# TensorE transposes one pair of edge tiles ahead instead of two (graph attention and expert layer, one core)

## The chip, the core and the metric

The kernel runs on one NeuronCore of a Trainium2 chip. TensorE (PE in the rows, PEld its weight loads) multiplies matrices into PSUM, VectorE is DVE, ScalarE is ACT, GpSimd is POOL, SyncE is SP. The time is the device time of one execution in microseconds, the median of several runs. Lower is better.

## What is computed

A graph network with three layers of message passing over 3125 nodes and 50000 edges, then a mixture of 8 experts over the nodes. Nearly all of the time that matters here goes into the messages of the three layers:

```
Q, K, V = (h @ Wq.T + bq), (h @ Wk.T + bk), (h @ Wv.T + bv)      # 4 heads of 64, for each node
scores  = einsum('ehd,egd->ehg', Q[src], K[tgt]) / 8             # 4x4 for each edge
attn    = softmax(scores, axis=-1)
msg     = einsum('ehg,egd->ehd', attn, V[tgt]) + Ee[edge_type]
proj    = msg @ Wo.T + bo
m       = segment_sum(proj, src)                                 # by source node
h       = relu(layer_norm(h + m, ln_g, ln_b))
```

## The kernel before, in words

The kernel sorts the edges by source node once. It groups them in tiles of 128 edges whose sources lie in one window of 16 nodes. `kv_d` in HBM holds a row of 512 numbers per node: 256 of K and 256 of V. In each of the three layers the edge phase (`e_phase`) walks over all tiles, two tiles (a **pair**) at a time. There are 294 pairs in a layer, 882 in all. Twelve pairs make a **turn** (`PAIRS` = 12). The first and the last turn are written out, and the turns between are a hardware loop on every engine. The last turn is a half one with 6 pairs, so a layer has 24 turn ends, 72 in all.

The order of the work on each engine is written out by hand, and semaphores tie the engines together. For a pair p:

- **POOL** gathers the 128 rows of each of its two tiles from `kv_d` into `kv` with two indirect DMAs (L527). `kv` holds 12 pairs. So the gathers of the next turn's pair p may start only after the aggregation of this turn's pair p (`agg_done`).
- **PE, `keys`** (L1463 to L1469) waits for `gathered` and transposes the K half of both tiles into bank 3 + p % 2: 4 transposes. It raises `kT_done`.
- **ACT, `keys`** (L1242 to L1245) copies that bank to `kt_s[:, p % 2]` and raises `kT_ready`. Behind it in ACT's order stand the four small copies of `queries` for the next pair (L1239, L1240), and after every fourth pair the exponentials of a group of four pairs (`exps`, L1249), which wait for DVE.
- **PE, `scores`** (L1471 to L1483) first multiplies a bf16 mask into bank p % 3 (L1474), then waits for `kT_ready` and multiplies `kt_s` by the block diagonal queries `qbd`: 4 products (L1481). It raises `score_done`.
- **DVE** takes maxima (`best`, L763), and for a group of four pairs makes the softmax. It spreads the weights to `att` (L789), and adds the result of the aggregation to the window's sums `acc` (`add`, L806).
- **PE, `aggregate`** (L1485 to L1494) multiplies the V half of the tiles by `att`: 8 products into bank 5 + p % 3. It runs 7 pairs behind the scores (`LAG` = 7) and raises `agg_done`, for which DVE's `add` and POOL's gathers wait.

An fp32 product is two matmul records in the trace, so a pair counts 1 mask product, 8 scores records and 16 aggregation records; the 4 transposes count 4.

The loop over pairs in PE's `turn` (L1502 to L1509) is where the change is. In the kernel before, `keys` for pair p + 1 stands ahead of `aggregate` and `scores` of pair p. Before the first turn stands `keys(0)` (L1511).

Of the kernel before, what the change touches and what calls it, by code (L numbers as in the profile page):

```python
# [49 lines left out]
PAIRS = TILES // 2  # L50
# [3 lines left out]
LAG = 7  # L54
# [29 lines left out]
def build(nc, A, out):  # L84
    ctx = ExitStack()
    with ctx:
# [1291 lines left out]
        def _(pe):  # L1378
# [83 lines left out]
            def e_phase(l):  # L1462
                def keys(p, landed):  # L1463
                    for t in (2 * p, 2 * p + 1):
                        pe.wait_ge(gathered[t], landed)
                        for c in range(KC):
                            o = (t % 2) * D + c * P
                            ins = pe.transpose(bank[3 + p % 2][:, o:o + P], kv[:, t // UB, t % UB, c * P:(c + 1) * P], ident[:, :])  # L1468
                    ins.then_inc(S.kT_done, 1)  # L1469

                def scores(i, p, at):  # L1471
                    bk = bank[p % 3]
                    pe.wait_ge(S.score_read, at[p + 1])
                    mm(bk[:, :], ohT[:, ds(i * (PAIRS // 4) + p // 4, 1), :].squeeze(1),  # L1474
                       maskc[:, 2 * (p % 4):2 * (p % 4) + 2, :].unsqueeze(2).to_broadcast([P, 2, H, DH]),
                       start=True, stop=False, skip_group_check=True)
                    pe.wait_ge(S.kT_ready, at[p])
                    for u in range(2):
                        for c in range(KC):
                            o = u * D + c * P  # L1480
                            ins = mm(bk[:, o:o + P], kt_s[:, p % 2, u, c, :], qbd[:, p % 4, u, :],  # L1481
                                     start=False, stop=(c == KC - 1), skip_group_check=True)
                    ins.then_inc(S.score_done, 1)  # L1483

                def aggregate(p, weights, read):  # L1485
                    pe.wait_ge(S.att_ready, weights)
                    pe.wait_ge(S.chain_b, read)
                    for g in range(H):
                        for t in (2 * p, 2 * p + 1):
                            b, u, r = t // UB, t % UB, t % 2 * DH  # L1490
                            ins = mm(bank[5 + p % 3][r:r + DH, 0:DH], kv[:, b, u, D + g * DH:D + (g + 1) * DH],  # L1491
                                     att[:, b % 2, u, :, g, :],
                                     start=(g == 0), stop=(g == H - 1), skip_group_check=True)
                    ins.then_inc(S.agg_done, 1)  # L1494

                def turn(i, first, last):
                    pairs = LASTP if last else PAIRS
                    at = [pe.snap(l * EP + i * PAIRS + p + 1) for p in range(pairs + 1)]
                    read = [pe.snap(l * EP + i * PAIRS + p) for p in range(pairs)]
                    here = [pe.snap((l * (NTURN - h) + i + 1) * 16) for h in range(2)]  # L1500
                    ahead = pe.snap((l * NTURN + i + 2) * 16)
                    for p in range(pairs):  # L1502
                        if p + 1 < pairs:
                            keys(p + 1, here[(p + 1) * 2 // PAIRS])
                        elif not last:
                            keys(0, ahead)
                        if p >= LAG or not first:
                            aggregate((p - LAG) % PAIRS, at[p], read[p])
                        scores(i, p, at)  # L1509

                keys(0, pe.snap((l * NTURN + 1) * 16))  # L1511
                turn(0, True, False)
# [294 lines left out]
```

## Time and profile before

| | |
|---|---|
| time, median of 3 runs | 4428.94 us (4425.26 to 4429.85) |
| span of the profiled execution | 4428.6 us |
| PE busy | 3650.6 us, 82% of the span |
| DVE busy | 2620.2 us, 59% |
| POOL busy | 2316.9 us, 52% |
| ACT busy | 2195.7 us, 50% |
| three edge phases | 953, 951 and 952 us, from their first to their last scores |
| DMA in the edge phases | 161 GB/s, 58% of the 16 engines |

The profiled execution is as long as the median run. The three edge phases are 2856 us of it, 3.24 us for each of the 882 pairs. PE is recorded as busy for about 83% of an edge phase. Its matmuls overlap each other in the records, and the record of one tells when it was issued and a modelled end.

### The profile page before, as it was taken

The numbers are of one execution on the slowest core, as the hardware profiler recorded it, in microseconds if no ns is written. First come the engines' busy times: TensorE is split into PE (matmuls) and PEld (weight loads), VectorE is DVE, ScalarE is ACT, GpSimd is POOL, SyncE is SP. The second block draws the span as 40 slices with busy tenths as digits, with TensorE's granted clock in tenths as the row PEclk, the third lists the DMA queues.
The fourth block names the chain that finished last, engine by engine and source line by source line (L and its number), as shares of the span: only waits on it lengthen the run. The fifth ranks groups of instructions, "written<-read, shape, count | busy, mean of one in ns | idle before, by whom it ended". The sixth has DMA issues, their size and how long they took to land.

```text
span 4428.6 us, 98340 instructions
## 1 busy us (share of the span) xinstructions
PE 3650.6 (82%) x32539; PEld 2873.4 (65%) x32540; DVE 2620.2 (59%) x6787; ACT 2195.7 (50%) x6662; POOL 2316.9 (52%) x2354
## 2 busy tenths in 40 slices
PE   5777878888888887888888888788888888868999
PEld 2333547676766664776667676567666667657998
DVE  6555626676666753666667665367666667661111
ACT  3667755454444434554445543455544445323443
POOL 2555225666666633566666663356666666334444
PEclk9777889999999988999999998899999999888999
DMA  2000145555555534555555553455555555436665
GB/s 65 0 0 0 39 156 145 163 162 162 163 163 161 163 95 151 150 161 163 161 164 163 163 161 94 137 157 161 163 163 163 163 162 162 131 108 186 186 181 127
DMA packets 231295, 611.20 MB, mean 138 GB/s; under 512 B 52352, under 2 KB 96269, under 8 KB 222862
## 3 DMA queue, kind: packets, MB, share of 16 engines
q0 software_dynamic: 161376, 477.59, 39.7%
q1 hardware_dynamic: 69822, 132.43, 8.9%
q8 instruction: 46, 0.75, 0.1%
q14 instruction: 51, 0.42, 0.0%
HBM read 562.97 MB, written 47.19 MB: 138 GB/s over the span
## 4 chain that ended last, share of the span: by engine, by line
PE 75%; issue 13%; DVE 6%; another core or an unknown queue 3%; DVEq 1%; ACT 1%; DMA 1%; SPq 0%; POOL 0%; ACTq 0%; POOLq 0%
PE bank L1481 19%; PE bank L1491 15%; PE bank L1468 9%; PE bank L1474 6%; PE bank L1680 5%; PE bank L1692 4%; PE bank L1452 3%; PE bank L1525 2%; PE bank L1404 2%; PE bank L1418 2%; PE bank L1446 2%; PE bank L1412 1%; PE bank L1420 1%; PE bank L1526 1%
## 5 line engine op out<-in xcount | busy, mean ns | idle before, releaser
L527 POOL DMA_INDIRECT arena<-kv_d,gidx x1764 | 1754.7, 995 | 1283.2 <-PE bank L1491 541.5
L1481 PE MATMUL bank<-qbd,kt_s 128*128 128x128 f32 x7056 | 1063.7, 289 | 173.2 <-issue 119.9
L1481 PEld LDWEIGHTS bank<-qbd,kt_s 128*128 128x128 f32 x7056 | 1014.2, 203 | 261.5 <-issue 183.1
L1244 ACT ACTIVATE kt_s<-bank 128x512 f32<-128x512 f32 x882 | 523.7, 594 | 1207.3 <-PE bank L1468 583.9
L1491 PE MATMUL bank<-att,arena 128*64 128x64 f32 x14112 | 777.2, 237 | 275.0 <-issue 227.9
L763 DVE TENSOR_REDUCE sc<-bank 128x32 f32<-128x512 f32 x882 | 610.0, 692 | 661.4 <-remote 331.9
L1491 PEld LDWEIGHTS bank<-att,arena 128*64 128x64 f32 x14112 | 588.0, 144 | 493.4 <-issue 449.9
L789 DVE TENSOR_TENSOR att<-at_s,arena 128x512 f32<-128x512 f32 x882 | 610.8, 692 | 57.8 <-DVE at_s L782 23.8
L1468 PE MATMUL bank<-ident,arena 128*128 128x128 f32 x3528 | 586.2, 286 | 68.8 <-issue 41.8
L806 DVE TENSOR_TENSOR arena<-bank,arena 64x64 f32 x1764 | 393.6, 223 | 222.0 <-issue 85.0
L1468 PEld LDWEIGHTS bank<-ident,arena 128*128 128x128 f32 x3528 | 444.8, 149 | 98.4 <-issue 86.9
L1239 ACT ACTIVATE qbd<-arena 64x64 f32 x1764 | 441.5, 250 | 56.2 <-issue 45.7
L1240 ACT ACTIVATE qbd<-arena 64x64 f32 x1764 | 449.4, 255 | 20.5
L511 POOL DMA_INDIRECT rec_d<-arena x241 | 242.9, 1008 | 255.7 <-DVE arena L713 184.8
L1474 PE MATMUL bank<-maskc,arena 128*128 128x512 bf16 x882 | 358.0, 406 | 22.4 <-issue 21.9
L699 DVE CUSTOM_DVE_ANT_0 arena<-bank,arena 128x200 f32<-128x200 f32 x391 | 138.5, 363 | 176.5 <-PE bank L1418 88.2
L1151 DVE TENSOR_TENSOR arena<-bank,arena 128x256 f32<-128x256 f32 x56 | 23.8, 425 | 357.5 <-PE bank L1692 357.5
L1680 PE MATMUL bank<-xT,arena 128*128 128x128 f32 x1792 | 211.9, 277 | 0.0
L1680 PEld LDWEIGHTS bank<-xT,arena 128*128 128x128 f32 x1792 | 207.2, 194 | 0.4 <-ACT xT L1359 0.4
L1412 PE MATMUL bank<-arena 128*128 128x200 bf16 x391 | 112.7, 299 | 112.9 <-DVE rank L699 78.7
L1692 PE MATMUL bank<-arena 128*128 x896 | 202.6, 379 | 0.0
L1171 ACT ACTIVATE arena<-arena 128x592 bf16<-128x592 f32 x150 | 105.1, 776 | 176.1 <-DVE arena L716 168.6
(239 smaller groups left out, 3845.4 us busy)
## 6 DMA issues: line engine op xcount, KB each, us to landing
arena<-in_pack SPq DMA_DIRECT2D x56, 1030.0 KB
arena<-kv_d,gidx POOLq DMA_INDIRECT x1764
kv_d<-arena SPq DMA_DIRECT2D x50, 256.0 KB, 2.0
xin<-hid_d SPq DMA_DIRECT2D x75, 128.0 KB
arena<-in_w SPq DMA_DIRECT2D x8, 1024.0 KB, 6.1
kv_d<-arena SPq DMA_DIRECT2D x5, 1280.0 KB, 5.3
hid_d<-arena SPq DMA_DIRECT2D x50, 128.0 KB, 2.0
rec_d<-arena POOLq DMA_INDIRECT x241
```

The costliest lines, as they stand in the source:

```text
L527: pool.indirect_dma_start(kv[:, t // UB, t % UB, :], None, kv_d, bass.IndirectOffsetOnAxis(gidx[:, h, t - h * HT:t - h * HT + 1], 0),).the ...
L763: dve.tensor_reduce(sc[:, 2 * m:2 * m + 2], bank[q % 3][:, :].rearrange("p (t g s h) -> p t g h s", t=2, g=H, s=W), AX.X, ALU.max).then_in ...
L789: dve.tensor_tensor(att[:, b, u:u + 2].rearrange("p t s g h -> p t s (g h)"), at_s[:, 2 * m:2 * m + 2].rearrange("p t g h -> p t (g h)").u ...
L806: dve.tensor_tensor(a.rearrange("p (h s) -> p h s", h=H), bank[5 + p % 3][u * DH:(u + 1) * DH, 0:DH].rearrange("p (s h) -> p h s", h=H), a ...
L1239: act.activation(qbd[0:DH, p % 4, u, 0:64], q, ACT.Copy)
L1240: act.activation(qbd[DH:P, p % 4, u, 64:128], q, ACT.Copy)
L1244: act.activation(kt_s[:, p % 2], bank[3 + p % 2][:, :].rearrange("p (u c n) -> p u c n", u=2, n=P), ACT.Copy).then_inc(S.kT_ready, 1)
L1468: ins = pe.transpose(bank[3 + p % 2][:, o:o + P], kv[:, t // UB, t % UB, c * P:(c + 1) * P], ident[:, :])
L1474: mm(bk[:, :], ohT[:, ds(i * (PAIRS // 4) + p // 4, 1), :].squeeze(1), maskc[:, 2 * (p % 4):2 * (p % 4) + 2, :].unsqueeze(2).to_broadcast( ...
L1481: ins = mm(bk[:, o:o + P], kt_s[:, p % 2, u, c, :], qbd[:, p % 4, u, :], start=False, stop=(c == KC - 1), skip_group_check=True)
L1491: ins = mm(bank[5 + p % 3][r:r + DH, 0:DH], kv[:, b, u, D + g * DH:D + (g + 1) * DH], att[:, b % 2, u, :, g, :], start=(g == 0), stop=(g = ...
L1680: ins = mm(bank[1 + 2 * (p % 2) + h // 4][:, (h % 4) * P:(h % 4 + 1) * P], w1s[:, p, c * HID + h * P:c * HID + (h + 1) * P], xT[:, p % 2, ...
```

## The change

PE's loop over the pairs now takes `aggregate` and `scores` first and `keys` last. All three calls, their operands, banks and semaphore waits are the same as before, and so are the other engines' programs.

```
--- before.py
+++ after.py
@@ -1500,13 +1500,13 @@
                     here = [pe.snap((l * (NTURN - h) + i + 1) * 16) for h in range(2)]
                     ahead = pe.snap((l * NTURN + i + 2) * 16)
                     for p in range(pairs):
+                        if p >= LAG or not first:
+                            aggregate((p - LAG) % PAIRS, at[p], read[p])
+                        scores(i, p, at)
                         if p + 1 < pairs:
                             keys(p + 1, here[(p + 1) * 2 // PAIRS])
                         elif not last:
                             keys(0, ahead)
-                        if p >= LAG or not first:
-                            aggregate((p - LAG) % PAIRS, at[p], read[p])
-                        scores(i, p, at)
 
                 keys(0, pe.snap((l * NTURN + 1) * 16))
                 turn(0, True, False)
```

The first place is inside the hardware loop on PE, between two pairs. `gathered4` and `gathered5` are the landings of pair 2's tiles, `kT_ready` is ACT's copy of the transposed keys. Before, from the transposes of pair 2 on, the next products are:

```order
L1468 MATMUL bank<-ident,arena 128x128 [waits gathered4]
L1468 MATMUL bank<-ident,arena 128x128
L1468 MATMUL bank<-ident,arena 128x128 [waits gathered5]
L1468 MATMUL bank<-ident,arena 128x128
L1491 MATMUL bank<-att,arena 64x64 [waits chain_b,att_ready]
L1491 MATMUL bank<-att,arena 64x64 x7
L1473 REGISTER_ALU
L1474 MATMUL bank<-maskc,arena 128x512 [waits score_read]
L1481 MATMUL bank<-qbd,kt_s 128x128 [waits kT_ready]
L1481 MATMUL bank<-qbd,kt_s 128x128 x3
```

The scores in these rows are those of pair 1, so the scores of pair 2 come one whole round later. After, from the transposes of pair 1 on:

```order
L1468 MATMUL bank<-ident,arena 128x128 [waits gathered2]
L1468 MATMUL bank<-ident,arena 128x128
L1468 MATMUL bank<-ident,arena 128x128 [waits gathered3]
L1468 MATMUL bank<-ident,arena 128x128
L1491 MATMUL bank<-att,arena 64x64 [waits chain_b,att_ready]
L1491 MATMUL bank<-att,arena 64x64 x7
L1473 REGISTER_ALU
L1474 MATMUL bank<-maskc,arena 128x512 [waits score_read]
L1481 MATMUL bank<-qbd,kt_s 128x128 [waits kT_ready]
L1481 MATMUL bank<-qbd,kt_s 128x128 x3
```

The round reads the same, but here the transposes are those of pair 1 (`gathered2`, `gathered3`), like the scores. The transposes have moved behind the previous pair's scores, and only one aggregation and one mask product stand between a pair's transposes and its scores.

The second place is the start of a layer on PE. Before, two pairs are transposed ahead of the first scores:

```order
L1468 MATMUL bank<-ident,arena 128x128 [waits gathered0,oht_copied]
L1468 MATMUL bank<-ident,arena 128x128
L1468 MATMUL bank<-ident,arena 128x128 [waits gathered1]
L1468 MATMUL bank<-ident,arena 128x128
L1468 MATMUL bank<-ident,arena 128x128 [waits gathered2]
L1468 MATMUL bank<-ident,arena 128x128
L1468 MATMUL bank<-ident,arena 128x128 [waits gathered3]
L1468 MATMUL bank<-ident,arena 128x128
L1474 MATMUL bank<-maskc,arena 128x512 [waits score_read]
L1481 MATMUL bank<-qbd,kt_s 128x128 [waits kT_ready]
L1481 MATMUL bank<-qbd,kt_s 128x128 x3
```

After, the first scores follow the first pair's transposes directly:

```order
L1468 MATMUL bank<-ident,arena 128x128 [waits gathered0,oht_copied]
L1468 MATMUL bank<-ident,arena 128x128
L1468 MATMUL bank<-ident,arena 128x128 [waits gathered1]
L1468 MATMUL bank<-ident,arena 128x128
L1474 MATMUL bank<-maskc,arena 128x512 [waits score_read]
L1481 MATMUL bank<-qbd,kt_s 128x128 [waits kT_ready]
L1481 MATMUL bank<-qbd,kt_s 128x128 x3
L1468 MATMUL bank<-ident,arena 128x128 [waits gathered2]
L1468 MATMUL bank<-ident,arena 128x128
L1468 MATMUL bank<-ident,arena 128x128 [waits gathered3]
L1468 MATMUL bank<-ident,arena 128x128
```

Here the transposes of pair 1 (`gathered2`, `gathered3`) have moved behind the scores of pair 0.

## Rows read from the trace of the kernel before

**Rows 1.** The page: busy time by engine, and the costliest group of instructions.

```profile
PE 3650.6 (82%) x32539; PEld 2873.4 (65%) x32540; DVE 2620.2 (59%) x6787; ACT 2195.7 (50%) x6662; POOL 2316.9 (52%) x2354
...
L527 POOL DMA_INDIRECT arena<-kv_d,gidx x1764 | 1754.7, 995 | 1283.2 <-PE bank L1491 541.5
```

**Rows 2.** Windows, the edge phases: length, busy us by engine, clock, DMA share, GB/s.

```profile
639.00:1592.00 953.00, 789.26 (x8400) 660.08 (x8399) 644.11 (x1512) 467.25 (x1582) 581.14 (x582) 0.93 0.58 161
...
2846.00:3798.00 952.00, 781.83 (x8402) 651.02 (x8401) 643.60 (x1509) 465.79 (x1581) 575.41 (x582) 0.95 0.57 161
```

**Rows 3.** Line 527, POOL's gathers: what ended POOL's idle time (us, times).

```profile
  PE bank L1491: 541.5, 311
  issue: 484.2, 1382
...
  remote: 125.3, 70
```

**Rows 4.** Line 1244, ACT's copy of the keys: what it waited for (us, times).

```profile
  PE bank L1468: 583.9, 240
  remote: 578.4, 224
```

**Rows 5.** Timeline around two pairs that pass undisturbed: start, duration, idle before.

```profile
1508.58 1.05 PE L1481 MATMUL bank<-qbd,kt_s 128*128 128x128 f32 x8
...
1509.47 0.60 PE L1468 MATMUL bank<-ident,arena 128*128 128x128 f32 x4
...
1510.00 0.69 PE L1491 MATMUL bank<-att,arena 128*64 128x64 f32 x16
...
1510.11 0.60 ACT L1244 ACTIVATE kt_s<-bank 128x512 f32<-128x512 f32 x1 [0.28 <-issue]
...
1510.62 0.39 PE L1474 MATMUL bank<-maskc,arena 128*128 128x512 bf16 x1
1510.84 1.05 PE L1481 MATMUL bank<-qbd,kt_s 128*128 128x128 f32 x8
```

**Rows 6.** Timeline of a stretch with a late copy.

```profile
1446.59 1.05 PE L1481 MATMUL bank<-qbd,kt_s 128*128 128x128 f32 x8
...
1447.48 0.60 PE L1468 MATMUL bank<-ident,arena 128*128 128x128 f32 x4
...
1448.01 0.69 PE L1491 MATMUL bank<-att,arena 128*64 128x64 f32 x16
...
1448.96 0.38 PE L1474 MATMUL bank<-maskc,arena 128*128 128x512 bf16 x1 [0.26 <-issue]
1449.17 0.60 PE L1481 MATMUL bank<-qbd,kt_s 128*128 128x128 f32 x4
...
1450.39 0.62 PE L1481 MATMUL bank<-qbd,kt_s 128*128 128x128 f32 x4 [0.61 <-issue]
...
1451.84 0.69 DVE L763 TENSOR_REDUCE sc<-bank 128x32 f32<-128x512 f32 x1 [3.66 <-PE bank L1481]
...
1453.26 0.60 ACT L1244 ACTIVATE kt_s<-bank 128x512 f32<-128x512 f32 x1 [5.87 <-PE bank L1468]
```

**Rows 7.** Timeline of POOL alone: the gathers that come after a wait.

```profile
1201.97 1.05 POOL L527 DMA_INDIRECT arena<-kv_d,gidx  x1 [1.04 <-PE bank L1491]
...
1205.56 0.94 POOL L527 DMA_INDIRECT arena<-kv_d,gidx  x1 [1.28 <-PE bank L1491]
...
1212.11 0.94 POOL L527 DMA_INDIRECT arena<-kv_d,gidx  x1 [1.87 <-PE bank L1491]
```

**Rows 8.** Timeline of ACT at a turn's end.

```profile
835.15 0.60 ACT L1244 ACTIVATE kt_s<-bank 128x512 f32<-128x512 f32 x1 [0.24 <-issue]
836.88 0.26 ACT L1239 ACTIVATE qbd<-arena 64x64 f32 x1 [1.13 <-issue]
...
837.95 0.21 ACT L1233 ACTIVATE gidx<-rec 128x12 int32 x1
```

**Rows 9.** Line 1468, PE's transposes: idle time ended by a gather's landing (us, times).

```profile
  DMA arena<-kv_d,gidx: 32.9, 19
```

More of the change, by code:

```diff
@@ L1502, in turn @@
                     for p in range(pairs):
+                        if p >= LAG or not first:
+                            aggregate((p - LAG) % PAIRS, at[p], read[p])
+                        scores(i, p, at)
                         if p + 1 < pairs:
@@ L1506, in turn @@
                             keys(0, ahead)
-                        if p >= LAG or not first:
-                            aggregate((p - LAG) % PAIRS, at[p], read[p])
-                        scores(i, p, at)
                 keys(0, pe.snap((l * NTURN + 1) * 16))
```

## The prediction, made before the changed kernel ran

> **What bounds the kernel now.** I read the page first, then the windows of the three edge phases, then the waits of POOL and ACT, and last two timelines. No engine is full over the span: PE is recorded busy for 82% [rows 1]. The edge phases last 953 and 952 us, with the middle one 2856 us together, or 3.24 us for each of 882 pairs, and PE is busy in 789 of 953 [rows 2]. Where nothing disturbs it, one round is shorter: scores start at 1508.58 and again at 1510.84, so PE needs 2.26 us per pair [rows 5]. 882 x (3.24 - 2.26) = 864 us are lost in the edge phases.
>
> They are not lost where PE visibly waits for data: gather landings end only 32.9 us of idle time in front of the transposes [rows 9]. The late copies tell more. In the undisturbed round the transposes end at 1509.47 + 0.60 = 1510.07, and ACT's copy starts at 1510.11, 0.04 us later [rows 5]. In the other stretch the transposes end at 1448.08 and ACT, idle for 5.87 us, starts the copy at 1453.26, 5.2 us later. The scores that end at 1447.64 are read by an idle DVE only from 1451.84 [rows 6]. So PE's completion signals come late while POOL sends gathers one behind the other. Meanwhile PE's records run on: between the end of those scores and 1451.84 stand 4 + 16 + 1 + 8 matmuls [rows 6], one whole round, and the last of them trickle out with idle gaps of 0.6 us. I take it that PE can run about one round ahead of its own signals and then stands.
>
> With each of these matmuls goes a weight load, so the records are about 58. The Trainium skill ("TensorE: Matmul & The Clock Gate", What a matmul computes and Architectural detail) gives TensorE's queue a depth of 64; by that rule the trace agrees, and the run-ahead would end at 64 records where a dependency doesn't end it earlier.
>
> POOL shows the same from its side. Two gathers are 2 x 0.995 us [rows 1], its short gaps are 484.2 / 882 = 0.55 us per pair, and its waits for an aggregation (541.5 + 125.3 us in 381 times) are 0.76 us per pair [rows 3]: 3.30 us together, the 3.24 us within the rounding of what lies at the phases' ends. One wait comes per 882 / 381 = 2.3 pairs and lasts 1.75 us. So the edge phase beats in bursts: POOL waits, gets the aggregations that have become visible (two or three pairs), sends 4 to 6 gathers, PE's signals stay away meanwhile, and all begins again. How many aggregations a burst finds sets the pace.
>
> **What the change does, part by part.** It removes and adds no instruction. In the steady round the order of kinds stays transposes, aggregation, mask, scores. What moves is the pair: the transposes of a pair run one round, 2.26 us, later against its scores.
>
> (a) The copy in an undisturbed round. Before, from the end of a pair's transposes to its scores there are 2.26 + (1510.84 - 1510.07) = 3.03 us; now 0.77 us. The copy needs 0.04 + 0.60 = 0.64 us [rows 5]. It fits with 0.13 us to spare: the cover is the aggregation and the mask. Cost 0. If the cover is gone (a busy ACT, a late signal), each us of it is a us of PE.
>
> (b) The copy in a disturbed round. Before, a pair's transposes could be hidden from ACT for up to 3.03 - 0.64 = 2.4 us without holding its scores; now for 0.13 us. ACT waited 583.9 + 578.4 us for 464 of 882 copies, 2.5 us each [rows 4]; this is not all lateness of the signal, since ACT is idle between copies anyway. The run-ahead of a whole round ends now at the first scores whose transposes have not become visible, that is after an aggregation and a mask. When the signals come, the copy has to run (0.64 us) before the next scores, and the aggregation behind these comes that much later, near the time when POOL's new gathers shut the signals off again. So a burst finds fewer aggregations. Nothing in the trace of before runs so; I bound it. Low end: the bursts stay as they are, 0. High end: each burst finds one pair. A burst of one pair takes 1205.56 - 1201.97 = 3.59 us [rows 7], against 3.24: 0.35 x 882 = 309 us. A burst of two takes 1212.11 - 1205.56 = 6.55 us [rows 7]. I take the middle, one and two pairs in turn: (3.59 + 6.55) / 3 = 3.38 us per pair, 0.14 x 882 = 124 us. I lean on this one because one aggregation is always in the run-ahead and the next comes about one round plus the copy later (2.9 us), about when a burst of two gathers (2 x 1.25 us) ends.
>
> (c) Turn ends. There ACT loads the windows' registers behind the copy: from the copy's start at 835.15 to the end of the last small operation, 837.95 + 0.21, are 3.01 us [rows 8], against a round of 2.26. The next copy is 0.75 us late, less the 0.13 to spare, where the round is undisturbed. Before, the extra round hid it. I take half, 0.3 us x 72 turn ends = 22 us; ends 0 and 45.
>
> (d) The softmax chain. The exponentials stand behind the copy and the four small copies on ACT, and the copy comes up to one round later. DVE's weights wait for them, and the aggregations wait for DVE's spread. They run 7 pairs behind, so I take 0; if the cover failed it would show as PE waiting at L1491 for L789. I leave up to 50 us for it in the high end.
>
> (e) Gains. The transposes come a round later against their gathers, which can return at most the 32.9 us [rows 9]; most of it lies at the layers' starts, where the landings set the pace in either order. I take 0; ends 0 and -33. The other stages are untouched.
>
> Sum, against the profiled execution (span 4428.6 us, 0.3 below the median 4428.94, so nothing to convert): 4428.6 + 124 + 22 = 4575 us.
>
> **Rivals.**
> One pair per burst: with only 0.13 us to spare every burst finds one aggregation. For it: it takes a signal just 0.13 us late to hold the scores. Against it: after a release two rounds can pass before the signals go (copies come at once in rows 5). 4429 + 309 + 22 = 4760; with (d) and copies that wait as in rows 6, up to 5000.
> The cover holds, not slower: signals are late because PE itself stands, and when it goes on, 0.77 us of aggregation and mask cover 0.64 us of copy just as in the undisturbed round. Then the lookahead was spare, and only (c) could be left. It decides at a copy path of 0.77 us: below it, nothing is lost. 4429, or 4451 with (c). For it: the same order of kinds, the clean round. Against it: the 5.2 us in rows 6.
> By the Trainium skill ("Perfetto Trace Analysis", Matmuls) independent groups should rotate through banks so that the evacuation of one overlaps the next group's products. That rule is still met after the change, and by it the time would be this rival's.
> A faster kernel: the later transposes never meet a gather that hasn't landed, and the first scores of a layer start earlier. 4429 - 33 = 4396. Against it: 19 such waits in 882 pairs [rows 9].
>
> **How the numbers follow.** Middle case 0.46 (4500 to 4660), one pair per burst or worse 0.26 (4660 to 5000), cover holds 0.18, faster 0.10. A difference below 0.2% (9 us) can't be told from none. The cover case gives 0.13 to no change and 0.05 to a small loss by (c), the faster case 0.01 to no change: faster 0.09, same 0.14, slower 0.77. Low end 4425, just at the no-change case; high end 4840, which leaves about 0.1 on each side.
>
> **What would show it.** Right: no change outside the edge phases, each some 50 us longer; more than 381 waits of POOL for an aggregation (near 590), each about as long; PE waiting at L1477's semaphore, idle in front of the scores with ACT's copy as its releaser; recorded run-ahead shorter than a round. (c) is right if intervals at turn ends are the longest. Wrong: POOL's waits as many as before and PE's idle time still in small gaps in the middle of a group; or PE waiting for L789, then (d) was the step. A lower granted clock than 0.93 in an edge phase [rows 2] would be an effect that I left out.

## The result, and the profile after

The changed kernel took 4496.81 us (median of 4 runs, 4491.84 to 4499.76), and the kernel before, on the same chip, 4429.4 us. The ratio is 1.0154, with a 95% interval from 1.0139 to 1.0169: 67 us slower. The forecast was 4575 us, 146 us slower. The sign, the place and the mechanism came out as predicted, the size at less than half of the forecast. The profiled execution of the changed kernel has a span of 4490.0 us, 61.4 more than before.

The page of the changed kernel, busy time by engine and the costliest group. These answer to [rows 1].

```profile
PE 3588.0 (80%) x32539; PEld 2796.1 (62%) x32540; DVE 2621.3 (58%) x6787; ACT 2213.6 (49%) x6662; POOL 2264.2 (50%) x2354
...
L527 POOL DMA_INDIRECT arena<-kv_d,gidx x1764 | 1698.0, 963 | 1404.3 <-PE bank L1491 673.2
```

Windows of the changed kernel: the three edge phases, from their first to about their last scores, against [rows 2] (length, busy us by engine, clock, DMA share, GB/s). The first two end 4.8 and 3.6 us before the last scores do.

```profile
634.00:1606.00 972.00, 765.38 (x8351) 627.37 (x8352) 641.84 (x1505) 471.24 (x1580) 561.83 (x583) 0.95 0.56 158
1761.00:2734.00 973.00, 761.85 (x8372) 626.86 (x8371) 642.91 (x1507) 471.29 (x1580) 559.99 (x581) 0.96 0.56 157
2885.00:3859.00 974.00, 769.04 (x8405) 629.83 (x8406) 644.13 (x1510) 473.62 (x1586) 559.53 (x583) 0.96 0.56 158
```

Counted in the two traces from the first to the start of the last scores, the phases are 23, 25 and 22 us longer, 70 us in all, or 3.32 us a pair in place of 3.24. Counted from a layer's first gather it is 65 us, since the first scores then start 0.7 to 2.3 us earlier (5 us in all). Outside the phases nothing became longer; the first gather came 3.4 us earlier, which leaves the 61.4 of the span. The granted clock is 0.95 and 0.96 where it was 0.93 to 0.95, so it isn't the clock. About 50 of the 65 us are spread over all the later turns (3.29 us a pair between the scores of pairs 12 and 288, before 3.23). Nearly all of the rest, 21 less the 5 that come back, comes in the first turn of each layer.

Now the waits of the same kernel. Line 527, POOL's gathers: what ended the idle time in front of them (us, times), against [rows 3].

```profile
  PE bank L1491: 673.2, 374
  issue: 463.3, 1309
  remote: 135.7, 80
```

Line 1481, PE's scores:

```profile
  ACT kt_s L1244: 529.2, 672
  issue: 320.4, 152
```

Line 1244, ACT's copy of the keys, against [rows 4]:

```profile
  remote: 929.2, 355
  PE bank L1468: 440.6, 487
```

POOL now waits 454 times for an aggregation, 808.9 us, where it waited 381 times, 666.8 us. That is 142 us more. Against it, its gathers are 56.7 us shorter (963 ns in place of 995) and its short gaps 20.9 us (463.3 against 484.2): 142.1 - 56.7 - 20.9 = 64.5 us, the lengthening of the phases counted from their first gathers. PE's idle time in front of the scores (matmuls and weight loads are two rows of the trace and are summed here) ended with ACT's copy 14 times before, for 91.2 us:

The kernel before, line 1481:

```profile
  issue: 303.0, 555
  ACT kt_s L1244: 91.2, 14
```

Now it does so 672 times. The rows don't tell where in a group of eight scores matmuls an idle time lies; the traces do (matmuls alone, idle over 0.15 us). Before, 196 of them, 103.5 us, lay inside a group and only 9, 53.8 us, in front of a group and up to the copy's end. After the change none lies inside a group, and 390, 350.6 us, end within 0.15 us of the copy's end, those that the row calls "issue" among them. The idle time has changed its form as the prediction said: PE no longer runs ahead until its records trickle out, it stands in front of the scores.

The timeline of the changed kernel shows one such round. Columns are start, duration, operation and, in brackets, the idle time before it with its releaser.

```profile
1451.15 0.60 PE L1468 MATMUL bank<-ident,arena 128*128 128x128 f32 x4
...
1451.68 0.69 PE L1491 MATMUL bank<-att,arena 128*64 128x64 f32 x16
...
1452.30 0.10 PEld L1474 LDWEIGHTS bank<-maskc,arena 128*128 x1
1452.30 0.39 PE L1474 MATMUL bank<-maskc,arena 128*128 128x512 bf16 x1
1452.42 1.20 POOL L527 DMA_INDIRECT arena<-kv_d,gidx  x1 [0.30 <-issue]
1452.73 0.60 ACT L1244 ACTIVATE kt_s<-bank 128x512 f32<-128x512 f32 x1 [1.83 <-PE bank L1468]
...
1453.38 1.16 PE L1481 MATMUL bank<-qbd,kt_s 128*128 128x128 f32 x8 [0.69 <-issue]
```

The transposes end at 1451.75, the copy starts 0.98 us later though ACT has been idle for 1.83 us, and the scores follow the copy's end by 0.05 us after PE has stood for 0.69 us. (The row says "issue", but nothing else ends there; only the copy does.) This signal was less late than most; how late they are is counted further down.

### The profile page after: what moved, and what is told of

It is laid out like the page before. It is cut to its first block, busy times and chain, and to the rows that moved or that the text cites. A ratio compares the mean times of both kernels' runs of the same rounds, so it can differ in the third digit from the quotient of the medians.

```text
span 4490.0 us, 98340 instructions
## 1 busy us (share of the span) xinstructions
PE 3588.0 (80%) x32539; PEld 2796.1 (62%) x32540; DVE 2621.3 (58%) x6787; ACT 2213.6 (49%) x6662; POOL 2264.2 (50%) x2354
## 4 chain that ended last, share of the span: by engine, by line
PE 51%; another core or an unknown queue 18%; ACT 13%; issue 9%; DVE 4%; ACTq 3%; DMA 0%; DVEq 0%; SPq 0%; POOL 0%; POOLq 0%
PE bank L1481 14%; PE bank L1468 6%; ACT kt_s L1244 5%; PE bank L1680 5%; PE bank L1692 4%; PE bank L1491 3%; ACT qbd L1240 3%; ACT qbd L1239 3%; PE bank L1452 3%; PE bank L1404 2%; PE bank L1525 2%; ACTq L1259 2%; PE bank L1474 2%; PE bank L1446 2%
## 5 line engine op out<-in xcount | busy, mean ns | idle before, releaser
L527 POOL DMA_INDIRECT arena<-kv_d,gidx x1764 | 1698.0, 963 | 1404.3 <-PE bank L1491 673.2
L1481 PE MATMUL bank<-qbd,kt_s 128*128 128x128 f32 x7056 | 1027.5, 291 | 354.5 <-ACT kt_s L1244 203.4
L1481 PEld LDWEIGHTS bank<-qbd,kt_s 128*128 128x128 f32 x7056 | 900.5, 199 | 520.8 <-ACT kt_s L1244 325.8
L1491 PE MATMUL bank<-att,arena 128*64 128x64 f32 x14112 | 734.1, 235 | 268.8 <-issue 244.3
L1491 PEld LDWEIGHTS bank<-att,arena 128*64 128x64 f32 x14112 | 566.9, 142 | 455.6 <-issue 443.3
L1468 PE MATMUL bank<-ident,arena 128*128 128x128 f32 x3528 | 555.4, 282 | 22.0 <-DMA arena<-kv_d,gidx 22.0
L778 DVE TENSOR_REDUCE sm<-ex 128x32 f32<-128x128 f32 x222 | 83.5, 376 | 199.7 <-ACT ex L1249 186.1
```

Source lines behind the costliest of these rows:

```text
L527: pool.indirect_dma_start(kv[:, t // UB, t % UB, :], None, kv_d, bass.IndirectOffsetOnAxis(gidx[:, h, t - h * HT:t - h * HT + 1], 0),).the ...
```

## The experiments

Sixteen runs followed, of the change once more and of eleven variants. They landed on chips that differ by far more than the change, so each is set against the kernel before on its own chip:

| kernel | order of a pair, or edit | before there | this | ratio (95%) |
|---|---|---|---|---|
| the change | A S(p) K(p+1) | 4429.4 | 4496.81 | 1.0154 (1.0139 to 1.0169) |
| after_2 | the same again | 4431.58 | 4502.49 | 1.0163 (1.0139 to 1.0188) |
| e1_aks_2 | A K(p+1) S(p) | 4431.58 | 4438.11 | 1.0014 (1.0004 to 1.0023) |
| e7_ahead | A K(p+2) S(p) | 4429.86 | 4433.61 | 1.0010 (0.9999 to 1.0021) |
| e8_ahead_exps | e7, exponential earlier | 4429.86 | 4435.11 | 1.0010 (1.0000 to 1.0020) |
| e11_sak | S(p) A K(p+1) | 4509.88 | 4809.45 | 1.0654 (1.0636 to 1.0672) |
| e2_split_2 | the change, copy in halves | 4429.86 | 4528.48 | 1.0232 (1.0214 to 1.0249) |
| e3_exps_2 | the change, exponential earlier | 4429.86 | 4507.90 | 1.0182 (1.0161 to 1.0203) |
| e4_load_2 | the change, register load earlier | 4509.88 | 4583.77 | 1.0162 (1.0134 to 1.0189) |
| e5_half_after | the change, rows of half the size | 4431.58 | 4485.54 | 1.0129 (1.0112 to 1.0145) |
| e6_half_before | before, rows of half the size | 4431.58 | 4432.96 | 1.0002 (0.9992 to 1.0013) |
| e9_plain_after | the change, plain transfers | 4509.88 | 3897.84 | 0.8644 (0.8628 to 0.8660) |
| e10_plain_before | before, plain transfers | 4509.88 | 3892.77 | 0.8627 (0.8613 to 0.8642) |
| e1_aks | A K(p+1) S(p) | 3764.31 | 3757.46 | 0.9975 (0.9965 to 0.9985) |
| e2_split | as e2_split_2 | 3764.31 | 3762.99 | 0.9993 (0.9979 to 1.0008) |
| e3_exps | as e3_exps_2 | 3764.31 | 3757.29 | 0.9972 (0.9961 to 0.9984) |
| e4_load | as e4_load_2 | 3764.31 | 3760.28 | 0.9983 (0.9972 to 0.9993) |

(A is the aggregate, S the scores, K the transposes, with the mask always in front of S. Before is K(p+1) A S(p). The half-size rows and the plain transfers leave part of the work out, as said below.)

The theory under test, A: the change takes away lead, the work that stands on PE between the transposes of a pair and its scores, and this lead covered the late completion signals. Rivals: B, the softmax chain; D, the length of the copy; C, the aggregate's place; and the turn ends as a term of their own. The expectations of the first four use other letters: there B is the aggregate's place in e1_aks and the copy's length in e2_split, and C is the softmax chain. In after_2, B says that aggregation and mask are too short a cover on any chip. Later ones add A2 (late signals come from the indirect DMAs), E (they are a property of the chip, whatever POOL does) and F (what costs is that the scores stand behind the aggregate).

### The first four, on a chip where signals come at once

e1_aks puts the transposes between the aggregate and the scores:

```
 aggregate((p - LAG) % PAIRS, at[p], read[p])
+keys(p + 1, ...)
 scores(i, p, at)
-keys(p + 1, ...)
```

> Order aggregate(p-7), transposes(p+1), scores(p): the transposes stay ahead of the scores of the pair before, only the aggregation has moved ahead of them. Theory A (lookahead: the scores of a pair must not need transposes that have not yet become visible to ScalarE; the loss is the lost round of lookahead): nearly all comes back, 4420 to 4445 us, PE idle in front of L1481 for the copy under 150 us against 529 us. Theory B (the loss comes from the aggregation standing ahead of the transposes, which delays them against the gathers and ScalarE): it stays near 4497 us.

e2_split copies the keys of the two tiles apart (a helper that counted on the semaphore `spare` counts on another one here):

```
-act.activation(kt_s[:, p % 2], bank[3 + p % 2][:, :] ...).then_inc(S.kT_ready, 1)
+for u in range(2):
+    act.activation(kt_s[:, p % 2, u], bank[3 + p % 2][:, u * D:(u + 1) * D] ...).then_inc(S.kT_ready if u == 0 else S.spare, 1)
...
 for u in range(2):
+    pe.wait_ge(S.kT_ready if u == 0 else S.spare, at[p])
```

> The changed order, with the copy of the transposed keys in two halves, each with its own semaphore, so that the scores of the first tile start after half a copy (about 0.35 us after the signal in place of 0.60). Theory A (the signal of the transposes is what comes late, by up to 2 us): 4480 to 4500 us. Theory B (the 0.64 us of copy just doesn't fit under aggregation and mask, and after each late signal the whole copy is exposed): 0.25 us for each of the 672 waits at half weight comes back, 4440 to 4465 us.

e3_exps and e4_load move one operation of ACT each:

```
# e3_exps
 keys(p, at)
+if p % GP == 1 and (p > 1 or not first):
+    exps(GP, ...)
 queries(p + 1)
-if p % GP == 1 ...: exps(GP, ...)
# e4_load
+if p == pairs - 1 and not last:
+    act.load(areg, ...)
 keys(p, at)
 ...
 elif not last:
-    act.load(areg, ...)
     queries(0)
```

> The changed order, with ScalarE's exponentials of a group directly behind the copy, ahead of the four small copies of queries (1.04 us earlier). Theory C (the loss is VectorE's new wait for the exponentials, 186 us in 162 times, that reaches the aggregations): 4440 to 4465 us. Theory A: VectorE's wait shrinks but was slack, 4490 to 4505 us.

> The changed order, with ScalarE's register load at a turn's end ahead of the copy of the last pair's keys in place of behind it. My step (c) said 0.3 us for each of 72 turn ends: 22 us come back, 4475 us, if the load can wait its time out before the transposes' signal. Theory A alone: the turn end costs nothing of its own, 4490 to 4505 us.

Measured: 3757 to 3763 us, all within 0.3% of the kernel before, which took 3764.31 us on this chip, 15% less than where the change had been timed. So none of these tells the theories apart, and the reason is the finding. Here is POOL's line 527 of e1_aks:

```profile
  issue: 561.2, 1685
  ACT gidx L1233: 126.6, 3
  PE bank L1491: 23.2, 76
```

Timeline of e1_aks:

```profile
701.44 0.65 PE L1468 MATMUL bank<-ident,arena 128*128 128x128 f32 x4
...
702.15 1.05 PE L1481 MATMUL bank<-qbd,kt_s 128*128 128x128 f32 x8
702.15 0.95 POOL L527 DMA_INDIRECT arena<-kv_d,gidx  x1 [0.30 <-issue]
702.20 0.60 ACT L1244 ACTIVATE kt_s<-bank 128x512 f32<-128x512 f32 x1
...
703.41 0.94 POOL L527 DMA_INDIRECT arena<-kv_d,gidx  x1 [0.30 <-issue]
```

POOL sends one gather behind the other and hardly ever waits for an aggregation (23.2 us), and still the copy starts at once: the next operation of ACT begins 0.11 us after the transposes' end at 702.09, right behind its neighbour. In front of line 1481 no idle time at all is listed. Over the whole trace, ACT was idle at the end of a pair's transposes 711 times, and no copy started over 0.2 us after it. The same kernel, the same gathers, and no late signals. In e3_exps, with the lead cut as in the change, line 1481 waits 107.6 us for the copy in 213 times, and the time doesn't suffer. The change as such was not run on this chip; three variants that have its order of PE ran at 0.9972 to 0.9993.

### The same questions where signals come late

The change was run again beside e1_aks and a pair with half the bytes.

```
# e5_half_after, e6_half_before
-kv[:, t // UB, t % UB, :], None, kv_d, bass.IndirectOffsetOnAxis(gidx[...], 0),
+kv[:, t // UB, t % UB, 0:D], None, kv_d.rearrange("n (a d) -> (n a) d", a=2), bass.IndirectOffsetOnAxis(gidx[...], 0),
```

The half-size rows leave the V half of the tiles unloaded, and their K half is another row's.

> The changed kernel once more. The first experiments ran on a chip where the kernel before takes 3764 us in place of 4429, and where ScalarE's copy starts 0.309 us after the last transpose's start whenever ScalarE is free. Theory A (the lost lookahead costs only where TensorE's completion signals come late while GpSimd's gathers run): where before takes 3764 us, the change costs nothing, ratio 0.995 to 1.002, and TensorE shows no late copies; where before takes 4429 us, 1.0154 again. Theory B (the copy under aggregation and mask is too short a cover in any case): ratio 1.01 to 1.02 on either chip.

> The order aggregate(p-7), transposes(p+1), scores(p) again, to stand beside the changed kernel on one chip. Theory A: 0.997 of before, as in the first run, where signals are prompt; where they are late, 0.998 to 1.004, against 1.0154 for the changed kernel.

> The changed order, with each gather fetching rows of 1 KB in place of 2 KB (the V half of the tiles is not loaded and the K half is another row's), so with the same number of indirect DMAs and half their bytes. If late signals come from the bytes in flight, their lateness halves where they are late, and the kernel there takes at most 4100 us; if they come from GpSimd's issuing of indirect DMAs, it stays within 2% of 4497 us. Where signals are prompt, VectorE's 31.5 us per turn bounds, and it stays within 0.5% of the changed kernel.

> The order of before with the same half gathers. Where bytes in flight make the signals late: at most 4050 us; where the issuing does: within 2% of 4429 us. Where signals are prompt: within 0.5% of before, and within 0.3% of the changed order with half gathers.

Measured: the change 1.0163 again; e1_aks_2 1.0014, so two groups more between the transposes and the scores (three in place of one) give back 64 of the 71 us; half the bytes 1.0129 and 1.0002. Halving the bytes gives the changed kernel 17 us back of 71 and the kernel before nothing, so the bytes in flight are at most the small part. In e1_aks_2 line 1481 reads

```profile
  issue: 268.8, 389
  ACT kt_s L1244: 200.8, 207
```

between before (91.2) and the change (529.2, and 532.4 in after_2), and POOL's waits of line 527 are back at before's, 378 of them:

```profile
  PE bank L1491: 548.9, 320
  issue: 487.1, 1385
  ACT gidx L1233: 133.7, 1
  remote: 107.9, 58
```

The next four ran with the kernel before at 4429.86 us. In e7_ahead the lead is longer than it ever was, with the idle xT as a third buffer for the copied keys. The wait for the copy moves from `scores` to the place shown, and the transposes of pair 1 also stand ahead of the first turn:

```
 aggregate((p - LAG) % PAIRS, at[p], read[p])
+pe.wait_ge(S.kT_ready, at[p])
+keys(p + 2, ...)
 scores(i, p, at)
```

> The changed kernel, with ScalarE's copy of the keys in two halves, each with its own semaphore, and the scores of a tile waiting for its half alone. Of use only where the kernel before takes about 4430 us (there the changed kernel takes about 4500). Theory A (the scores wait for a copy that is released late, by TensorE's completion signal, and the copy's own length is the small part): 4480 to 4510, since both halves begin as late as before and only half a copy, some 0.3 us of the waits that end with it, is saved; the waits of L1481's line for ScalarE stay above 400 us in sum. Rival D (the length of the copy between the transposes and the scores is the cost): 4430 to 4465. Where the kernel before takes about 3764 us, no difference over 0.3% from 3760.

> The changed kernel, with ScalarE's exponential moved directly behind the copy of the keys, ahead of the queries' copies. Rival B (the later scores push the softmax chain, and the chain holds the aggregates): where the kernel before takes about 4430 us this gives back most of the 68 us, 4430 to 4460, and the waits of VectorE for the exponential fall from about 190 us to under 50. Theory A (TensorE waits for the copy of the keys, the chain has spare time): within 10 us of the changed kernel, 4490 to 4510, even if VectorE's waits fall. Where the kernel before takes about 3764 us: 3757, as the first time.

> The opposite of the change: the order within a pair is aggregate, transposes of the pair two ahead, scores, with a third buffer for the copied keys (the idle xT), and TensorE waits for the copy of pair p before it transposes p + 2. Four more groups, in place of three before and one now and a half, lie between the transposes of a pair and its scores. Theory A (what costs is how far the transposes run ahead of the scores, measured against a completion signal that comes late): where the kernel before takes about 4430 us, the waits of the scores' line for ScalarE are no longer than before's (about 90 us in sum) and the time is 4380 to 4435, not slower than before. Rival C (any placing of the aggregate ahead of the transposes costs, since it holds the turn's freeing of buffers and so the gathers): slower than before, 4460 or more. Where the kernel before takes about 3764: 3745 to 3770 by both.

> The kernel with the transposes two pairs ahead, and ScalarE's exponential directly behind its copy of the keys as well. Theory A: within 10 us of the kernel with the transposes two pairs ahead alone. Rival B (the softmax chain costs something in either order): 10 to 30 us faster than that one.

Measured:

- e2_split_2, 1.0232: by the ratios some 31 us worse than the change (1.0163), outside both expectations. D is refuted, and my own figure (4480 to 4510) as well. In the rows of line 1245 (its copies) a half takes 380 ns where the whole takes 597, but the two halves overlap, so that all take 580 us in place of 527 (0.66 us a pair), and line 1482 (its scores) waits longer than in the change (647.9 us in 467 times against 529.2). What makes it longer is not shown: a pair's copies end only 0.06 us later than the whole one did.
- e3_exps_2, 1.0182. The exponential does reach DVE earlier: VectorE's line 778 waited 186.1 us for it in the change, before 5.4, and now waits

```profile
  ACT ex L1249: 58.2, 90
```

  Yet nothing comes back: 4507.90 us, where B asked for 4430 to 4460. B is refuted: the wait appeared, as a by-product, and shortening it gains nothing.
- e7_ahead, 1.0010, with no idle time ended by ACT's copy in front of the scores any more, and only 10.1 us in 4 times in front of the transposes, where the wait now stands (four groups stood between transposes and scores before, five up to its wait here; the expectation's count is off). The aggregate stands ahead of the transposes, so C is refuted. And more lead than before buys nothing: what is left of POOL's waits, 648.2 us, isn't the copy's doing. The longer lead has a price too. The transposes now meet gathers that haven't landed, 161 times for 130.6 us (before 19 times, 32.9 us), so whether lead alone would have gained something isn't shown.
- e8_ahead_exps, the same.

### One more step down, turn ends, and where late signals come from

These four ran on a fourth chip, where the kernel before took 4509.88 us.

```
# e9_plain_after, e10_plain_before
-pool.indirect_dma_start(kv[:, t // UB, t % UB, :], None, kv_d, bass.IndirectOffsetOnAxis(gidx[...], 0)).then_inc(gathered[t], 16)
+pool.dma_start(kv[:, t // UB, t % UB, :], kv_d[rows(t), :]).then_inc(gathered[t], 16)
# e11_sak
+scores(i, p, at)
 aggregate((p - LAG) % PAIRS, at[p], read[p])
-scores(i, p, at)
 keys(p + 1, ...)
```

> The changed kernel with every indirect gather replaced by a plain transfer of 128 adjacent rows of the same table, of the same size, issued by GpSimd at the same place under the same waits; it leaves out the selection of the rows by the edges. Theory A2 (the completion signals of TensorE come late because GpSimd issues indirect DMAs at the same time): where the kernel before takes about 4430 us, the edge phases run at the pace seen on the chip where signals come at once (2.63 us a pair in place of 3.23), the time is 3850 to 4000, and the changed order and the former one differ by less than 15 us. Rival E (the late signals are a property of that chip, whatever GpSimd does): near 4500, and 50 us or more above the same kernel in the former order. Where the kernel before takes about 3764 us, no more than 30 us below that.

> The kernel before with the same replacement, leaving out the same. Theory A2: within 15 us of the changed order with plain transfers, 3850 to 4000 where the kernel before takes about 4430. Rival E: about 4430, 50 us or more under the changed order with plain transfers.

> The changed kernel with one step more taken from the lead of the transposes: scores, aggregate, transposes of the next pair, so that nothing stands between the transposes of a pair and its scores. Theory A: the cost grows as the lead falls (former order 0; aggregate, transposes, scores +7 us; the change +68): where the kernel before takes about 4430, 4600 to 4900, and the waits of the scores' line for ScalarE's copy go above 900 us. The aggregate no longer covers the copy, some 1.2 us a pair even where signals come at once, of which the slack of TensorE there (about 0.9 us a pair) hides most: 3764 to 4000 where the kernel before takes about 3764. Rival F (what costs is that the scores stand behind the aggregate of the same pair, and the lead plays no part): no slower than the changed kernel.

> The changed kernel with ScalarE's register load at a turn's end moved ahead of its copy of the last pair's keys. Theory A (turn ends play no part, as the trace of the changed kernel shows them no longer than other pairs): within 8 us of the changed kernel, about 4500 where the kernel before takes about 4430. My predicted term for the turn ends (0.3 us at each of 72): 15 to 25 us less than the changed kernel.

**e11_sak**, 1.0654: 300 us, and F is refuted. With nothing but the mask between transposes and scores, POOL's line 527 reads

```profile
  PE bank L1491: 1156.8, 810
  issue: 346.8, 938
  ACT gidx L1233: 129.1, 1
  remote: 23.4, 15
```

825 waits for 882 pairs: nearly every burst finds one pair. This is the prediction's high end of (b), 0.35 x 882 = 309 us from a burst of one [rows 7], and the timeline of e11_sak has the round of 3.59 us (1451.66 to 1455.25) that those rows gave:

```profile
1451.66 1.16 PE L1481 MATMUL bank<-qbd,kt_s 128*128 128x128 f32 x8 [1.05 <-ACT kt_s L1244]
1451.70 0.94 POOL L527 DMA_INDIRECT arena<-kv_d,gidx  x1 [1.42 <-PE bank L1491]
...
1453.36 0.66 PE L1468 MATMUL bank<-ident,arena 128*128 128x128 f32 x4
...
1454.60 0.60 ACT L1244 ACTIVATE kt_s<-bank 128x512 f32<-128x512 f32 x1 [1.74 <-PE bank L1468]
...
1455.25 1.16 PE L1481 MATMUL bank<-qbd,kt_s 128*128 128x128 f32 x8 [1.02 <-ACT kt_s L1244]
```

The time lies within the 4600 to 4900 of theory A, also when it is scaled to a kernel before of 4430 us (4720). The waits for the copy in front of the scores, foretold "above 900 us", are 2128.0 us, matmuls and weight loads summed, as the 529.2 were; the matmuls alone have 894.3.

Not all of this is the late signal. The copy itself has lost its cover as well. In e9_plain_after (below), where no signal is late, a round with only the mask between transposes and scores is 0.74 us longer than in the former order. My estimate for a clean round of e11_sak is therefore 2.26 + 0.74 = 3.00 us, and its signals are some 0.6 us late: 3.6, where the trace has 3.62 us a pair between the scores of pairs 12 and 288. So that it meets the 3.59 of [rows 7] may be chance, and no run has this order with prompt signals, to tell the two parts apart.

**e4_load_2**, 1.0162, the ratio of the change itself (1.0154 and 1.0163). The interval leaves room for a gain of up to some 11 us against the first of these, not for the 22 us of the term (c), if the change costs the same ratio on this chip, where it wasn't run. The interval between scores across a turn's end did become shorter, 3.32 us against the 3.72 of the change on its chip, without a gain in the whole.

**e9_plain_after and e10_plain_before**, 3897.84 and 3892.77 us: without the indirect DMAs the edge phase is as short as where signals come at once (the third one takes 768 us in e9_plain_after and 766 in e1_aks on its chip, by the windows below), and the two orders differ by 5 us, 0.13%. These two leave out the selection: they fetch the same adjacent rows in every turn. Windows of e9_plain_after and of e1_aks, third edge phase:

```profile
2490.00:3258.00 768.00, 673.63 (x8410) 587.50 (x8409) 643.95 (x1511) 472.09 (x1586) 309.69 (x581) 1.00 0.62 200
```

```profile
2362.00:3128.00 766.00, 723.33 (x8391) 600.60 (x8391) 644.82 (x1512) 469.18 (x1577) 584.82 (x579) 1.00 0.69 199
```

The timeline of e9_plain_after, with the changed order (its lines are shifted: 1466 transposes, 1489 aggregate, 1472 mask, 1479 scores, 1242 copy):

```profile
1201.93 0.60 PE L1466 MATMUL bank<-ident,arena 128*128 128x128 f32 x4
...
1202.46 0.69 PE L1489 MATMUL bank<-att,arena 128*64 128x64 f32 x16
1202.57 0.60 ACT L1242 ACTIVATE kt_s<-bank 128x512 f32<-128x512 f32 x1 [0.74 <-PE bank L1466]
...
1203.08 0.39 PE L1472 MATMUL bank<-maskc,arena 128*128 128x512 bf16 x1
1203.30 1.07 PE L1479 MATMUL bank<-qbd,kt_s 128*128 128x128 f32 x8
...
1203.73 1.07 POOL L527 DMA_DIRECT2D arena<-kv_d  x2 [1.22 <-PE bank L1489]
```

This is the undisturbed round of the prediction's step (a): the copy starts 0.04 us after the transposes, ends at 1203.17, and the scores come 0.13 us later. Against the late copy above, all of the lateness is gone. It is gone everywhere: ACT was idle at the end of the transposes 807 times in e9_plain_after and 223 times in e10_plain_before, and no copy started over 0.2 us after it. The same count gives 159 late copies of 334 before the change, 2.9 us late on average, and 353 of 810, 2.1 us, after it. And POOL waits 817 times, nearly once a pair, without harm:

```profile
L527 POOL DMA_DIRECT2D arena<-kv_d x1764 | 941.5, 539 | 1524.9 <-PE bank L1489 1297.2
```

The first pairs of a layer show what the change costs without any late signal. `aggregate` is left out there until pair 7, so the mask alone covers the copy. PE in e9_plain_after:

```profile
664.63 0.38 PE L1472 MATMUL bank<-maskc,arena 128*128 128x512 bf16 x1
665.49 1.16 PE L1479 MATMUL bank<-qbd,kt_s 128*128 128x128 f32 x8 [0.47 <-ACT kt_s L1242]
...
667.77 1.16 PE L1479 MATMUL bank<-qbd,kt_s 128*128 128x128 f32 x8 [0.47 <-ACT kt_s L1242]
```

and in e10_plain_before, in the former order:

```profile
673.29 1.05 PE L1479 MATMUL bank<-qbd,kt_s 128*128 128x128 f32 x8
...
674.84 1.05 PE L1479 MATMUL bank<-qbd,kt_s 128*128 128x128 f32 x8
```

A round takes 2.28 us in place of 1.54. From the scores of pair 0 to those of pair 12 it is 5 us more in each layer (30.0 against 24.9), and behind them the two orders have the same pace, 2.62 us a pair.

Reservations: a plain transfer also occupies POOL for 539 ns in place of about 980, the rows it reads are adjacent and not scattered, and the granted clock in the edge phase is 1.00, against 0.93 to 0.95 in the kernel before [rows 2]. Which of these goes with the prompt signals isn't taken apart. But e1_aks ran at full pace with scattered rows, gathers of 0.95 us and 0.30 us between them, so on that chip neither their length nor the scatter made a signal late; and a clock 5 to 7% higher is too little for rounds that are 19% shorter (2.62 in place of 3.24 us a pair).

## Where the prediction was right and where it failed

**What bounds the kernel.** Right. Late completion signals while POOL sends indirect gathers: taking the indirect form away (e9, e10) took 13.6% off the time and with it nearly all of the cost of the change. That the gathers hold the signals back shows in the traces as well: in the changed kernel 239 of the 353 late copies start 2.0 to 2.2 us after the start of the gather before them (83 of 159 before), and in e11_sak 758 of 793 at 1.6 to 1.7 us. The run-ahead of "about one round" was right too: while a copy was late, at most 63 records of PE followed the transposes before, and at most 34 after the change. That aggregations are found in bursts was right, but e9_plain_after shows that one pair per burst isn't a cost by itself.

**(a)** Right for the steady round: 0.77 us of cover against 0.64 us of copy, 0.13 us to spare, seen again to the hundredth in e9_plain_after. It overlooked the first seven pairs of each layer, which have no aggregation as cover and where the copy is exposed in every round.

**(b)** This is the step that failed, in its size and not in its mechanism. It gave 124 us as the middle between unchanged bursts and one pair per burst, and took bursts of one and two pairs in turn, near 590 waits of POOL. There are 454, and the later turns lengthened by 50 us. Counted in the traces from one wait for an aggregation to the next, 210 bursts before were of four gathers (two pairs), 117 of six and 34 of two; after the change 350 are of four, 16 of six and 66 of two. So the change turned bursts of three pairs into bursts of two, and those of two held. The bursts themselves last as long as before: 3.7, 6.5 and 9.6 us for one, two and three pairs, in both traces. With these, the mix before gives 3.23 us a pair and the mix after 3.28, that is 0.056 x 882 = 50 us.

The error was in the sentence "I lean on this one because one aggregation is always in the run-ahead and the next comes about one round plus the copy later (2.9 us), about when a burst of two gathers (2 x 1.25 us) ends": in 350 of 454 cases the second aggregation was found. The 5.2 us of [rows 6] are also one of the longer delays. Where ACT was idle at the transposes' end, the late copies were late by 2.9 us on average before, by 2.1 after the change and by 0.7 in e11_sak. My reading is that PE which stands isn't far ahead of its signals, so that less is hidden; I had taken the lateness as given, and it shrank with the lead, while more of the copies became late (159 of 334, 353 of 810, 793 of 866). Another row was left without a term: gathers 32 ns shorter and 21 us less of short gaps at POOL, 78 us that come back against 142 of longer waits.

**(c)** Wrong, 22 us too much. In the changed kernel the intervals between scores alternate within a turn between some 3.7 us (means of 3.58 to 3.74 by place in the turn) and some 2.9 (2.63 to 3.28), and the one across the turn's end is 3.72, no longer than its like. e4_load_2 gives nothing back. That the 0.75 us fall into an interval in which the scores wait for a late signal anyway is my reading.

**(d)** Right at 0. The wait that it spoke of did appear, DVE for the exponential, 186.1 us against 5.4, but as waiting at DVE, and e3_exps_2 shows that it costs nothing.

**(e)** Put at 0, and wrong by the first turns. At a layer's start the first scores do come 0.7 to 2.3 us sooner, 5 us in all, but the first turn then takes 21 us more, 7 in each layer. I had given it no term. Some 5 of the 7 us appear without late signals too (e9_plain_after against e10_plain_before), from the pairs that have only the mask as cover.

**The sum.** 4428.6 + 50 for (b) + 15 for the first turns and 0 for the rest, less the 3.4 us by which the first gather came earlier, is the 4490 of the trace, against 4428.6 + 124 + 22. (b) was 74 us too high and (c) 22, and the 15 of the first turns were missing.

**The rivals.** One pair per burst is real, but one step of lead further down (e11_sak, 810 + 15 waits, +300 us), and there the exposed copy adds to it. "The cover holds" is what happens without late signals: 1.0013 between e9 and e10. The rule of the Trainium skill on rotating banks ("Perfetto Trace Analysis", Matmuls), by which the time would have been this rival's, was met in every order and told nothing here, since what was short was the distance to the consumer and not the number of banks. So both ends of the range for (b) exist as kernels, and the change lies at about a fifth of the way, where I took two fifths.

**Still open.** Why signals come late on some chips and not on another, under the same gathers; whether the change itself costs anything on that chip; and why the lateness falls when PE stands. The ends of the matmuls in a trace are modelled, so the traces can't tell either whether the signal is late or the products themselves finish late.

**No better version.** Where signals come late none beats the kernel before (e7_ahead 1.0010). Where they come at once e1_aks and e3_exps are 0.25% faster. The large sum, 13.6%, is in how the rows are fetched, but e9 and e10 leave the selection of rows out and so are no replacement.

## What to carry to other kernels

Between a producer on PE and its consumer on PE through another engine, count the work that stands between them, not only whether the round trip fits in the clean round: on the chips with late signals the 4 groups of the kernel before were enough, 3 cost 0.1%, 1 cost 1.5%, 0 cost 6.5%, the exposed copy included. Look at the first rounds of a loop too, where some of the covering groups may be left out. When the middle between two bounds is taken for a feedback (late signals make PE stand, and PE that stands makes fewer late signals), count how often each burst length occurs before and ask which of them the change can shorten; here that was the longest kind alone. And before explaining a few per cent, look at whether the signal that ends a wait is late by itself: compare the end of the producer with the start of an idle consumer.

## What the runs showed of the hardware

- With indirect DMAs going out from POOL, ACT and DVE saw PE's completions late: of the copies for which ACT stood idle at the transposes' end, 353 of 810 came 2.1 us late on average in the changed kernel, and 159 of 334, 2.9 us, before. With plain transfers of the same bytes, also issued by POOL, none came late, the copy followed 0.04 us behind the transposes, and the kernel took 3893 us in place of 4510.
- Chips differ in this. The same program took 4429, 4430, 4432 and 4510 us in four sets of runs, and 3764 us on one chip, where POOL's indirect gathers ran back to back (median 0.95 us each, 0.30 us apart) and no idle time stood in front of the scores. The sorting stage too, which also uses indirect DMAs, ended sooner: the first gather came at 509.9 us of the span of e1_aks there, and at 631.1 for the same kernel where signals come late.
- Half-size rows in the gathers changed the time of the kernel before by 0.02%: its edge phase isn't bound by the bytes moved.
- A copy of 128x512 took 597 ns and one of 128x256 380 ns on ACT. Two halves in a row overlap and took 0.66 us together.
